# Two experts' products share a slot without value products, and none shares a slot with one

## The reference

```
x = x + 0.5 * ffn(layernorm(x))                    # x W^T + b + (x V_r) C^T
x = x + attn0(layernorm(x))                        # 16 heads of 8; see below
x = x + 0.5 * ffn(layernorm(x))
x = x + 0.5 * moe(layernorm(x))                    # run 0 of the experts
x = x + attn1(layernorm(x))                        # 16 heads of 8, block mask
x = x + 0.5 * moe(layernorm(x))                    # run 1 of the experts

attn0: x = ln(x); q, k, v = x Wq, x Wk, x Wv; q, k l2-normalised by head; state = q
       twice: state = softmax(state k^T) v;  then  x + (state Wo + bo)
attn1: softmax(q k^T / sqrt(8), masked) v, then Wo
moe:   softmax gate over 8 experts, top 2; each expert and one shared expert is
       (silu(x w1[e]) * (x w3[e])) w2[e], on the gated input; the results are added
```

## Time and profile before

| | |
|---|---|
| median of three runs | 3466.11 us (3464.27 to 3475.04) |
| the profiled execution | 3461.28 us |
| its span | 3459.5 us |
| PE busy | 3189.1 us, 92% |
| DVE busy | 2363.8 us, 68% |
| ACT busy | 2079.8 us, 60% |
| POOL busy | 1268.6 us, 37% |
| mean granted TensorE clock | 0.982 |

### The profile page before, as it was taken

How to read it: one execution, slowest core, us unless ns; L and a number is a source line. 1 busy time by engine, 2 the same in 40 slices (tenths; PEclk the granted TensorE clock), 3 DMA queues, 4 the chain that set the end, 5 groups by cost and what they waited for, 6 DMA issues and landing times.

```text
span 3459.5 us, 55301 instructions
## 1 busy us (share of the span) xinstructions
PE 3189.1 (92%) x19974; PEld 1660.8 (48%) x19974; DVE 2363.8 (68%) x5153; ACT 2079.8 (60%) x2689; POOL 1268.6 (37%) x2419
## 2 busy tenths in 40 slices
PE   5889998989999999999999999999999999998999
PEld 2445444444444444444444445444444444444557
DVE  2645675847678676767868676776867677775662
ACT  2464666656666666666666666666666666664442
POOL 3324242342524334243533434352343435222421
PEclk8999999989999999999999999999999999999999
DMA  1000000001110100110011011110101111000111
GB/s 42 4 29 5 32 4 32 29 4 35 32 35 29 32 9 30 35 32 35 30 32 35 5 35 32 35 32 30 35 5 35 32 35 32 32 29 5 61 33 35
DMA packets 81501, 96.88 MB, mean 28 GB/s; under 512 B 50544, under 2 KB 68400, under 8 KB 81104
## 3 DMA queue, kind: packets, MB, share of 16 engines
q1 hardware_dynamic: 81232, 93.35, 8.4%
HBM read 82.76 MB, written 4.78 MB: 25 GB/s over the span
## 4 chain that ended last, share of the span: by engine, by line
PE 51%; DVE 16%; ACT 13%; POOL 10%; issue 8%; SPq 1%; DMA 0%; ACTq 0%; DVEq 0%; POOLq 0%
PE ps L681 13%; ACT probs L812 12%; PE ps L698 12%; PE ps L753 7%; DVE negmax L1042 6%; PE ps L763 5%; PE ps L581 5%; PE ps L718 4%; PE ps L587 2%; PE ps L576 2%; DVE stats L909 1%; DVE X L930 1%; POOL qT L1244 1%; POOL xe L1267 1%; POOL qk L1200 1%
## 5 line engine op out<-in xcount | busy, mean ns | idle before, releaser
L812 ACT ACTIVATE probs<-ps 128x1024 f32<-128x1024 f32 x1536 | 1573.6, 1024 | 1004.4 <-PE ps L681 989.1
L1042 DVE TENSOR_REDUCE negmax<-ps 128x2 f32<-128x1024 f32 x1024 | 1249.4, 1220 | 413.6 <-PE ps L718 396.8
L681 PE MATMUL ps<-qT,kT 32*128 32x512 f32 x3072 | 771.9, 498 | 109.3 <-ACT probs L812 57.8
L698 PE MATMUL ps<-probs,v 128*32 128x512 f32 x6144 | 832.1, 614 | 0.0
L1267 POOL TENSOR_TENSOR xe<-xT_m,G 128x512 f32<-128x512 f32 x288 | 367.5, 1277 | 1058.9 <-PE ps L753 960.2
L753 PE MATMUL ps<-xe,w_sb 128*128 128x256 f32 x2304 | 650.0, 407 | 7.9 <-DVE hid L1101 4.0
L681 PEld LDWEIGHTS ps<-qT,kT 32*128 32x128 f32 x3072 | 286.2, 182 | 745.1 <-ACT probs L812 513.1
L718 PE MATMUL ps<-kT,qT 32*128 32x512 f32 x2048 | 515.7, 498 | 57.2 <-DVE negmax L1042 52.8
L753 PEld LDWEIGHTS ps<-xe,w_sb 128*128 128x128 f32 x2304 | 396.3, 191 | 177.1 <-issue 132.5
L1099 DVE SCALAR_TENSOR_TENSOR th<-th,ps 128x256 f32<-128x256 f32 x576 | 237.1, 412 | 217.7 <-ACT th L842 213.5
L842 ACT ACTIVATE th<-ps 128x256 f32<-128x256 f32 x576 | 221.3, 384 | 169.0 <-PE ps L753 158.5
(11 more groups left out here) (169 smaller groups left out, 2645.2 us busy)
## 6 DMA issues: line engine op xcount, KB each, us to landing
G<-gates_dram SPq DMA_DIRECT2D x96, 768.0 KB, 6.3
maxrow<-negmaxT SPq DMA_DIRECT2D x512, 2.0 KB
v<-v_tok SPq DMA_DIRECT2D x256, 18.0 KB, 1.9
X<-in_x SPq DMA_DIRECT2D x16, 256.0 KB, 2.9
out<-X SPq DMA_DIRECT2D x16, 256.0 KB, 2.3
w_sb<-in_w SPq DMA_DIRECT2D x1, 1152.0 KB, 6.8
w_sb<-in_w SPq DMA_DIRECT2D x1, 576.0 KB, 7.8
gates_dram<-gT SPq DMA_DIRECT2D x32, 18.0 KB
```

The lines of the kernel that those rows point to most:

```text
L681: nc.tensor.matmul(ps[:, B_ST + h, :], kT[a][rows, g * S + kc * P:g * S + (kc + 1) * P], qT[a][rows, g * S:(g + 1) * S], start=True, stop= ...
L698: ins = nc.tensor.matmul(ps[ROWS * j:ROWS * (j + 1), B_UT, :], v[:, at:at + ROWS], probs[:, n % QUADS, j, :], start=(kc == 0), stop=(kc == ...
L812: nc.scalar.activation(probs[:, quad % QUADS, j:j + 2, :], ps[:, B_ST:B_ST + 2, :], ACT.Exp).then_inc(sem["exp_done"], 1)
L1042: nc.vector.tensor_reduce(negative[:, tc, 2 * half:2 * half + 2], ps[:, B_SM:B_SM + 2, :], AX_X, ALU.max, negate=True).then_inc(sem["sm_re ...
```

## The change

`FULL` goes from 1.0 to 1.25. A filler may then lie beside another: 0.22 + 0.47 + 0.47 = 1.16. And a filler may not be put into a slot that holds a `pv` until it has waited 12 slots beyond its wanted position. Nothing is computed differently; the steps are the same, and only where they stand changes.

```diff
-FULL, OVER = 1.0, 1.35
+FULL, OVER = 1.25, 1.35
+
+APART = 12
...
+        valued = set()
         marks = sorted(self.marks, key=lambda m: m[:2], reverse=True)
         for pos, i, name, args in marks:
             if name in ("st", "pv"):
                 load[int(pos // 1)] = load.get(int(pos // 1), 0) + COST[name]
+            if name == "pv":
+                valued.add(int(pos // 1))
...
             pos, i, name, args = mark
+            due = pos
             key = (name,) + args
...
                 if now + COST[name] > (FULL if name in FILLERS else OVER):
+                    return None
+                if name in FILLERS and slot in valued and slot < due + APART:
                     return None
```

## The result

The changed kernel takes 3500.17 us (median of 4 runs) where the kernel before, on the same chip, takes 3469.09 us (4 runs): a ratio of 1.0092, with an interval of 1.0074 to 1.0111. It is slower by 0.9%. The forecast had it 22 us faster. The profiled execution takes 3499.0 us with a span of 3497.2 us, 37.7 us over the 3459.5 of before. The mean granted clock is 0.982 in both.

The account below looks back on a forecast made before the run. Slots were taken as bound by the round of `st` and exponents, not TensorE's work. Regular turns -12 us, sequence 3 -7, turns before it +3, tail -6: -22 us, a median of 3444 us, range 3412 to 3493.

Parts of the forecast that it names:

- the price of slots 72-83: Slots 72-83 of a regular turn: `m_down` parts leave, `p1_qkv` and `p1_op` come in; -0.2 us, between -2 and +2.
- The `m_down` that leave: Slots 72-83: 8 parts out, as two pairs, two beside `pv` and two beside `p0_qkv`; -4.8 us.
- The `p1_qkv` beside an `sm`: Slots 72-83: three share a slot with an `sm`, and the third waits for a bank; +2.0 us with its neighbour.
- The `p1_op` of slot 81: Slots 72-83: eight `p1_op` come in over four slots; +0.8 us in each of the two with `pv`.
- the rival that only shifts: Gains reappear as costs elsewhere, waits of slots 84-95 only move to 79-82; -4 us in all, chance 0.20.
- slots 8-15, 16-23, 36-59 and 84-95: Four stretches of a regular turn, forecast in this order at +1.5, +2.0, +1.2 and -3.0 us.
- the price of a pair: Two `m_gu` in one slot with `st` and `sm`: 2.36 to 2.40 us, so 0.65 to 0.70 over 1.70.
- slots 24-35: Stretch of a regular turn where 7 parts of `m_down` leave pairs and `pv` slots; -5.0 us.
- slots 60-71: Stretch of a regular turn: 8 parts of `m_down` in, 5 `m_gu` out, slots 64, 66, 70 grow; +3.0 us.
- slots 0-7: Stretch of a regular turn: two costs of +0.65, against a projection and two transpositions leaving `pv` slots; -0.5 us.
- The turn of sequence 3: It takes 205.6 us, 7 above a regular turn, for waits behind a late `p1_op` that now comes sooner; -7 us.
- the slower one: Rival: banks and DVE's order take the gain back, 0.55 us for each of 74 new pairs; +19 us, chance 0.26.

Follow-up runs that it names:

- ord_qkv: The changed kernel with the readers of the q, k, v products 0.6 slots sooner in DVE's order and nothing else: 3463.9 us, 1.0003 against the kernel before.
- only_room: The kernel before with FULL 1.25 alone, so fillers may still stand beside a `pv` at once (APART 0): 3583.2 us, 1.0339.
- before_qkv: The kernel before with only the readers of the q, k, v banks 0.6 slots sooner in DVE's order: 1.0009.
- ord_ffn: The changed kernel with the readers of the q, k, v banks and of `ffn_y` 0.6 slots sooner in DVE's order: 1.0017 against the kernel before.

## Why the prediction was wrong

**The step that failed is the price of slots 72-83**: -0.2, between -2 and +2; it measured +4.0 at full clock and +4.7 as a mean. Its terms, as they are written, give -4.8 + 2.0 + 0.8 + 0.8 = -1.2; the -0.2 holds 1.0 us that no term names. Against the bare slots (1.70 us, or 1.64 with a `pv`) the terms came out so, in the turn of sequence 8:

- The `m_down` that leave were priced well: slots 72 and 76 to 78 fall by 3.6 us, and in slots 74 and 79 they had made 0.5 and 0.9. That is 5.0, forecast 4.8.
- The `p1_qkv` beside an `sm` were priced from the earlier trace rows as one wait, +2.0 with the neighbour. The row has that wait once, in a place where the next slot has no fourth product. Here the fourth meets the same order again in slot 75, and slots 74 and 75 take 7.70 us, 4.4 over bare ones.
- The `p1_op` of slot 81 cost 0.8, as forecast. Those of slot 79 cost 2.3 and not 0.8, with the wait of 0.96 us for DVE in it, and those of slots 80 and 82 were put at nothing; they wait 1.2 us each for ACT, and the two slots grow by 1.9.

The rest, -0.4 us, are the `turn` and `p1_xt` that leave slots 75 and 81 (-0.8) and a `p0_qkv` that costs 0.4 more in slot 73. The forecast has, for the rival that only shifts, that the waits of slots 84-95 would move to 79-82. The trace says so too: it was a term of the forecast and no rival to it.

ord_qkv shows that DVE's order of the readers costs the 0.9%. It leaves all work and TensorE's whole order alone, and 2.7 us of slots 72-83 go: 1.9 in slots 73 to 76, 1.3 in slot 79, less 0.5 in slot 81. Another 0.8 goes on average that a lower clock had added behind the long waits there. only_room's slot 75 says the same with another bank in place of another order. The bound that the text gave for being wrong, slots 72-83 over 29 us, was crossed, and the other, slots 8-15 over 21.5, was not. Not shown is what the early `p1` steps cost by themselves: no run has them at their old place within the changed plan, and before_qkv shows only that the order alone does nothing. Nor does the order explain the gain that was forecast and did not come: with it mended, the regular turn is at +2.9 us at full clock, where -1.0 was forecast. Of the 3.9 between, 1.5 are slots 72-83 still, for the most part the waits for ACT, and most of the rest are the stretches named next as too kind.

**Right in kind and size:** slots 8-15, 16-23, 36-59 and 84-95, each within 0.4 us at full clock; the price of a pair (0.65 to 0.70, measured 0.66 in slots 56 and 94, 0.69 in slot 8); the wait in slot 12 (1.08 us plus what follows it, forecast up to 1.4); POOL's 1.08 us in slot 87, whose slot falls from 3.16 to 2.51. **Too kind:** slots 24-35 gave 4.1 and not 5.0; slots 60-71 cost 4.2 and not 3.0: slot 64 grew by 2.4 where 1.1 and a wait of 0.5 to 1 had been put down, and slot 60 by 0.7, for which nothing had been, since its `m_gu` now waits 0.49 us for DVE; slots 0-7 cost 0.6 where 0.5 was to be gained (the terms as written give -0.3), and 0.6 of it is slot 2, whose `m_gu` waits 0.28 us for DVE. The turn of sequence 3 fell by 4.2, not 7. Of these only slot 64 was taken up in an experiment: ord_ffn takes 1.3 us out of it.

**Of the rivals,** the slower one ended on the right side, 19 us above before for a measured 31 to 38. Its mechanism, a side bank whose reader stands behind the maxima in DVE's order, is the one that was shown. But it had it at the wrong steps: it charged 0.55 us to each of 74 pairs of `m_gu`, and of the seven slots with a pair in the turn (0, 8, 10, 12, 42, 56, 94) only in slot 12 does an `m_gu` wait longer than 0.2 us for its bank. Their mean is 0.30 us over 2.36, above the 0.22 that the rival named as the point where it decides, but 1.46 of these 2.09 us is slot 12, which the sum had in it. The two that matter more are `p1_qkv`. A chance of 0.26 for it was too low for another reason, which the sum itself shows: taken as plain slot lengths the change had nothing to give. By its own prices each of the 98 more pairs of `m_gu` costs 0.65, 64 us, and the slot emptied for it gives back nothing; the 62 fillers moved off `pv`, at 0.98, give 61. The whole forecast of -12 for the regular turns hung on waits that would go.

**The rule of the Trainium skill** (TensorE: Matmul & The Clock Gate, section Back-to-back issue gap) of some 81 ns for each matmul of 128 columns does not hold here either. In slot 64 of the changed kernel ten loads take 1.19 us, 0.12 each, as in the earlier trace rows.

## What to carry to other kernels

Before a step is moved forward, look up which bank it will take, who reads that bank last, and what stands ahead of that reader in the reader's own fixed order; if that is something which waits for the engine that is being served, the two wait for each other, and the place in the reader's order can cost more than the move saves (0.9% here). A filler beside another is not free where the slot is paced by another engine: here the first was hidden, the second cost 0.66 us, and the slot that it left did not get shorter. And read the granted clock slot by slot before a difference of some us is put down to order or load.

## What the runs showed of the hardware

I had read the clock only as a mean (0.982 in both), and taken turns of 198.5 to 202.3 us in before for scatter. They are the clock, which goes between two levels, 2.4 GHz and 1.2 GHz. only_room's slots 15 and 16 in the turn of sequence 6, then slots 14, 15 and 16 in that of sequence 8:

```profile
1194.26:1196.78 2.52, 1.93 (x14) 0.53 (x14) 2.49 (x4) 1.02 (x1) 1.93 (x8) 1.00 0.00 0
1196.78:1200.80 4.02, 4.02 (x35) 3.34 (x31) 2.13 (x5) 1.02 (x1) 0.00 (x0) 1.00 0.00 0
1611.12:1613.40 2.28, 1.14 (x7) 0.70 (x6) 2.16 (x10) 1.51 (x2) 0.99 (x6) 1.00 0.04 11
1613.40:1617.08 3.68, 3.09 (x14) 0.68 (x14) 3.01 (x4) 1.02 (x1) 1.93 (x8) 0.59 0.01 2
1617.08:1623.65 6.57, 6.57 (x34) 5.91 (x31) 1.80 (x4) 1.02 (x1) 0.00 (x0) 0.50 0.00 0
```

Slot 16 holds 18 loads of `m_down` and takes 4.02 us at 1.00 and 6.57 at 0.50, the lower level throughout. Ahead of the fall TensorE was busy 1.14 of 2.28 us in slot 14. only_room falls there in eight of eleven turns, 4 us each; its mean turn is 211.2 us for 207.0 and 207.4 at a clock of 1.00, so that some 25 us of its loss (3.8 a turn, less the 1.5 that before loses in the same way, 11 times; an estimate) is the clock. after loses 0.7 a turn, nearly always behind its waits in slots 74 and 75, and ord_qkv none. A wait of TensorE thus costs twice at times: once itself, and once in the slots after it. The Trainium skill, TensorE: Matmul & The Clock Gate, section Part 1: The HAM clock gate, says that a monitor sets the clock by how busy the engine has been recently, and the runs agree: with the wait of slot 10 filled, the clock fell behind it in none of 33 turns. What no run explains is why the same slots with the same busy time keep the clock in one turn and lose it in the next, nor why two pairs of products in slot 6 made it fall in nine turns and not in five.
